# Moving the split of the second attention's query weights on GpSimd behind the first attention's last output product

## The chip, the core and the metric

The kernel runs on one core of a Trainium2 chip. A core has five engines with instruction streams of their own: TensorE (PE, matrix products, with weight loads listed as PEld), VectorE (DVE), ScalarE (ACT), GpSimd (POOL) and SyncE (SP, which issues the DMAs). They meet only in semaphores: an instruction waits until a counter has reached a number. The metric is the device time of one execution in microseconds (us), lower is better; a figure for a kernel is the median of several executions.

## What is computed

Two layers, each a cross attention and a feed-forward block, on 8 sequences of 128 tokens with 128 channels, and a context of the same length with 96 channels. Everything is float32.

```python
def reference(x, ctx_768, ...):
    x = x + _L0_xattn_ref(_layernorm(x), ctx_768, ...)   # 8 heads of 64
    x = x + _L0_ffn_ref(_layernorm(x), Wg, W1, W2, W3)   # 8 experts, top 2, silu(x W1) * (x W2) @ W3
    x = x + _L1_xattn_ref(_layernorm(x), ctx_768, ...)   # 16 heads of 8, with biases
    x = x + _L1_ffn_ref(_layernorm(x), k0, k1, k2, ...)  # three layers of +1/-1 weights
    return x
```

## The kernel before

Every engine has its program written out by hand, in order; there is no scheduler. The tokens lie in `x_sb` as eight blocks of 128 rows, one per sequence, and the blocks make two halves of 512 tokens. A product that needs full precision is made of three passes: weights and activations are each split into a rounded high part and a low rest, and `split3` multiplies high by high, high by low and low by high (lines 478 to 480). Splitting weights is GpSimd's work: a copy that rounds, then a subtraction of the copy from the raw weights.

The first attention (`a_step`) handles the blocks in four pairs, p = 0 to 3. In each step TensorE makes the next pair's queries (lines 478 to 480) and scores (L544), turns the probabilities (L555), multiplies them by the values (L566) and by the output weights (L575, which counts `a_wo` up once per block). VectorE takes the maxima (L1294), divides the probabilities by their sums (L1306) and adds the result to `x_sb` (L1312). ScalarE makes the exponentials (L983). The steps p = 1 and 2 are a hardware loop. `a_q_ps` counts query products, two for each pair, so it reaches 2 * NP = 8 when the last pair's queries are done, early in step p = 2. That is the "third pair" of this document.

Between the first attention and the experts lies the layer norm of both halves. For the first half VectorE seeds the inverse root and GpSimd refines it (`ln_root(1, 0)` on GpSimd, ten operations on 128x4 numbers, L344 to L354). For the second half all of it is on VectorE: moments (L1179), seed (L1186 to L1188), refinement (L1208 to L1215), and the scaling of the four blocks (L1220, `xn`). TensorE then turns them (`ln_transposes(1, 1)`, L485), ScalarE copies the high part (L950), VectorE makes the low part (L1227). On TensorE the order after the last output product is: `b_hidden(0, 0, 0)` (12 products), `gate_logits(0)`, `ln_transposes(1, 1)`, then a wait for `split_w1` at 4, `k1_keys(0)`, six filler products (`keep_clock`, L469), a wait for the second half's low part, `gate_logits(1)`, `k1_keys(1)`, and the experts.

`split_repeated(wq1, wq1_hi, wq1_lo)` is the piece that the change touches. It splits the query weights of the second attention and repeats them in a stacked layout: a rounding copy (L380), a subtraction (L381), and two memsets of 128x128 each (L382, L383). Each waits for the one before through `pool_step`, and the last one raises `split_w1` to 4. The destination is the first attention's own query weights, `wq1_hi, wq1_lo = wq0_hi, wq0_lo`, hence the wait for `a_q_ps` ahead of it. Three places read what it leaves: TensorE's wait before `k1_keys(0)`, VectorE's `stack_bias` (L1285), and the query products of the second attention. In GpSimd's program it stands behind the conversion of the weights `d1_w` and `d2_w` (L424, L425) and ahead of `ln_root(1, 0)`; then comes a wait for `a_wo` at 8, and the split of the third expert's weights (`split_expert`, L415 and L418), which waits for the experts' own progress as well.

Of the kernel before, what the change touches and what calls it, by code (L numbers as in the profile page):

```python
# [27 lines left out]
NP = NB // 2  # L28
# [20 lines left out]
def f32(ap):  # L49

    return ap.bitcast(F32)


def program(nc, a, out):
    with ExitStack() as ctx:
        def sb(name, shape, dt=F32):
            return ctx.enter_context(nc.sbuf_tensor(name, shape, dt))

        def sem(name):
            return ctx.enter_context(nc.semaphore(name))  # L60
# [63 lines left out]
        wq1 = sb("wq1", [C, C])  # L124
        wq1_hi, wq1_lo = wq0_hi, wq0_lo
# [90 lines left out]
        def o_cols(b):  # L216
# [19 lines left out]
        a_q_ps, a_qe, a_qo, a_s, a_max, a_exp, a_pt_ps, a_pt_v, a_pt_a, a_o, a_rs, a_norm, a_oT, a_wo, a_x = (  # L236
            sem("a_" + n) for n in ("q_ps", "qe", "qo", "s", "max", "exp", "pt_ps", "pt_v", "pt_a", "o", "rs", "norm",
                                    "oT", "wo", "x"))
# [14 lines left out]
        def stacked(ap):  # L253

            return ap[:, :].rearrange("c (h d p) -> c h p d", p=NS, d=D1)

        def repeated(ap):

            return ap[:, :].rearrange("c (h d) -> c h d", d=D1).unsqueeze(2).to_broadcast([ap.shape[0], H1, NS, D1])
# [68 lines left out]
        def _(pool):  # L328
            step = [0]

            def chain(ins):

                step[0] += 1
                ins.then_inc(pool_step, 1)
                pool.wait_ge(pool_step, step[0])

            def ln_root(s, t):


                pool.wait_ge(ln_seed, s + 1)  # L340
                bs = slice(4 * t, 4 * t + 4)
                v, y, h, z = ve[:, bs], rs[:, bs], nt[:, bs], nu[:, bs]

                chain(pool.tensor_tensor(h, y, y, ALU.mult))  # L344
                chain(pool.tensor_tensor(h, h, v, ALU.mult))
                chain(pool.tensor_scalar(z, h, -10.0 / 3, None, ALU.add))
                chain(pool.tensor_tensor(z, z, h, ALU.mult))
                chain(pool.tensor_scalar(z, z, 5.0, None, ALU.add))
                chain(pool.tensor_tensor(y, z, y, ALU.mult))

                chain(pool.tensor_tensor(h, y, y, ALU.mult))
                chain(pool.tensor_tensor(h, h, v, ALU.mult))
                chain(pool.tensor_scalar(h, h, -0.5 * 0.375 ** 3, 1.5 * 0.375, ALU.mult, ALU.add))
                pool.tensor_tensor(y, h, y, ALU.mult).then_inc(ln_rs, 1)  # L354
# [24 lines left out]
            def split_repeated(w, hi, lo):  # L379
                chain(pool.tensor_copy(stacked(hi), repeated(w)))  # L380
                chain(pool.tensor_tensor(stacked(lo), repeated(w), stacked(f32(hi)), ALU.subtract))  # L381
                chain(pool.memset(stacked(f32(hi))[:, :, NS - 1, :], 0.0))  # L382
                pool.memset(stacked(f32(lo))[:, :, NS - 1, :], 0.0).then_inc(split_w1, 1)  # L383
# [39 lines left out]
            pool.wait_ge(ld_d, 16 * 6)  # L423
            pool.tensor_scalar(d1_w[:, :, :], k1_u[:, :, :], 2.0, -1.0, ALU.mult, ALU.add).then_inc(d_w, 1)  # L424
            pool.tensor_scalar(d2_w[:, :, :], k2_u[:, :, :], 2.0, -1.0, ALU.mult, ALU.add).then_inc(d_w, 1)  # L425
            pool.wait_ge(a_q_ps, 2 * NP)
            split_repeated(wq1, wq1_hi, wq1_lo)
            ln_root(1, 0)

            pool.wait_ge(a_wo, NB)  # L430

            for buf in range(2):
                split_expert(2 + buf, buf)
# [1176 lines left out]
```

## Time and profile before

| what | value |
|---|---|
| median of 3 runs | 238.93 us |
| lowest and highest | 237.75 and 240.07 us |
| the profiled execution | 237.79 us, of which the span is 235.3 us |
| TensorE busy in the span | 221.6 us (94%) |
| VectorE, ScalarE, GpSimd busy | 165.6, 122.5 and 70.7 us |
| granted TensorE clock, mean | 1.00 |

The span is the time from the first to the last instruction on the chip; the profiled execution took 2.5 us more than its span. Times in the views count from the start of the span. A timeline row gives the start, the length, the engine, the line, the output and its inputs, how many instructions are merged, and in brackets how long the engine had been idle before it and what released it. The chain view follows the work that ended last back through whatever released each piece. "Busy" of an operation runs from when its engine took it up, so time for which it was held while on its engine is inside its length and shows as a longer row, not as idle time.

### The profile page before, as it was taken

To read this page: it belongs to the slowest core of one execution; us is meant where nothing else is said; L and a number is where in the kernel's file an instruction comes from. 1 tells how busy PE (TensorE), PEld (TensorE's weight loads), DVE (VectorE), ACT (ScalarE), POOL (GpSimd) and SP (SyncE) were. 2 spreads that over 40 slices of the span, in tenths; PEclk is the share of its full clock that TensorE was granted. 3 is DMA by queue.
4 is the path that set the end of the run, shared out by engine and by line. 5 is a ranking of instruction groups with operands and counts; after the bars stand their busy time and mean duration, and the time that the engine had idled before them with its cause. 6 is when DMAs were issued, how large, how long until landed. Compare 5 with 4: busy or idle time off the path is not lost.

```text
span 235.3 us, 5028 instructions
## 1 busy us (share of the span) xinstructions
PE 221.6 (94%) x1825; PEld 185.4 (79%) x1825; DVE 165.6 (70%) x429; ACT 122.5 (52%) x292; POOL 70.7 (30%) x105
## 2 busy tenths in 40 slices
PE   8999989798899999999999999999799999989994
PEld 8778879687787888898898889877578887766783
DVE  1688757778767796546555657988878889598763
ACT  2566869688583553323322324164456565757742
POOL 5626599533410215433033900251000000220200
PEclk9999999999999999999999999999999999999999
DMA  6870001000000002202202072000000000000002
GB/s 164 225 197 5 1 3 46 3 0 0 3 0 0 3 1 67 70 0 67 58 9 67 25 198 71 0 4 0 0 3 3 3 0 3 0 3 0 1 0 89
DMA packets 11868, 8.18 MB, mean 35 GB/s; under 512 B 3012, under 2 KB 11144, under 8 KB 11848
## 3 DMA queue, kind: packets, MB, share of 16 engines
q1 hardware_dynamic: 11848, 7.91, 12.6%
q8 instruction: 13, 0.21, 0.4%
q14 instruction: 7, 0.06, 0.1%
HBM read 5.81 MB, written 0.52 MB: 27 GB/s over the span
## 4 chain that ended last, share of the span: by engine, by line
PE 77%; DVE 10%; ACT 8%; issue 2%; POOL 0%; DVEq 0%; ACTq 0%; POOLq 0%
PE ps L676 11%; PE ps L478 9%; PE ps L480 9%; PE ps L850 9%; PE ps L479 9%; ACT probs L983 6%; PE ps L795 3%; PE ps L767 3%; PE ps L754 3%; DVE probs L1306 3%; PE ps L469 3%; PE ps L575 3%; PE ps L474 2%; PE ps L555 2%; PE ps L485 2%
## 5 line engine op out<-in xcount | busy, mean ns | idle before, releaser
L1038 ACT ACTIVATE kT<-ps 128x512 f32<-128x512 f32 x32 | 19.1, 598 | 47.0 <-PE ps L480 47.0
L676 PEld LDWEIGHTS ps<-w,kT 128*128 128x128 f32 x256 | 30.9, 192 | 1.3
L676 PE MATMUL ps<-w,kT 128*128 128x128 f32 x256 | 31.0, 275 | 0.0
L1376 DVE TENSOR_TENSOR kT<-ps,kT 128x512 f32<-128x512 f32 x32 | 21.8, 688 | 11.0 <-PE ps L480 8.7
L1383 DVE SCALAR_TENSOR_TENSOR x_sb<-ps,comb,x_sb 128x128 f32<-128x128 f32 x64 | 18.0, 343 | 13.5 <-PE ps L676 13.5
L478 PE MATMUL ps<-xT_hi,w_hi 128*128 128x512 f32 x64 | 26.5, 414 | 0.8 <-issue 0.6
L480 PE MATMUL ps<-xT_hi,w_lo 128*128 128x512 f32 x64 | 25.2, 394 | 0.0
L479 PE MATMUL ps<-xT_lo,w_hi 128*128 128x512 f32 x64 | 25.0, 391 | 0.0
L983 ACT ACTIVATE probs<-ps,negmax 128x128 f32<-128x128 f32 x64 | 22.6, 410 | 1.8 <-DVE negmax L1294 1.8
L415 POOL TENSOR_TENSOR w_hi<-w_raw,zero 128x512 fp32r<-128x512 f32 x8 | 9.3, 1168 | 46.2 <-DMA w_raw<-in_L_ffn_W 30.9
L1470 DVE TENSOR_REDUCE probs<-ps 128x8 f32<-128x1024 f32 x16 | 19.4, 1222 | 4.8 <-PE ps L754 4.7
L1084 ACT ACTIVATE probsT<-ps 128x1024 f32<-128x1024 f32 x16 | 16.5, 1029 | 9.7 <-PE ps L767 9.7
L460 POOL TENSOR_TENSOR h_a<-kT,h_a 128x512 fp32r<-128x512 f32 x2 | 2.6, 1282 | 46.8 <-ACT kT L1132 46.8
L983 ACT ACTIVATION_READ_ACCUMULATOR probs<-ps,negmax 128x1 f32 x64 | 16.1, 251 | 0.0
L478 PEld LDWEIGHTS ps<-xT_hi,w_hi 128*128 128x128 f32 x64 | 12.1, 188 | 3.2 <-issue 0.7
L480 PEld LDWEIGHTS ps<-xT_hi,w_lo 128*128 128x128 f32 x64 | 12.0, 188 | 2.7
L479 PEld LDWEIGHTS ps<-xT_lo,w_hi 128*128 128x128 f32 x64 | 12.1, 189 | 2.1
L1294 DVE TENSOR_REDUCE negmax<-ps 128x8 f32<-128x1024 f32 x8 | 9.7, 1221 | 5.6 <-PE ps L544 5.6
L1306 DVE TENSOR_TENSOR probs<-probs,rsum 128x1024 f32<-128x1024 f32 x8 | 11.6, 1452 | 0.3
L994 ACT ACTIVATE probsT<-ps 128x512 f32<-128x512 f32 x12 | 6.8, 613 | 9.5 <-PE ps L555 9.5
L754 PE MATMUL ps<-k_st,h_c 32*128 32x128 f32 x128 | 9.8, 276 | 1.4 <-DVE probs L1470 1.3
L555 PE MATMUL ps<-ident,probs 128*128 128x128 f32 x64 | 8.6, 278 | 2.4 <-DVE probs L1306 1.9
(207 smaller groups left out, 511.9 us busy)
## 6 DMA issues: line engine op xcount, KB each, us to landing
w_raw<-in_L_ffn_W SPq DMA_DIRECT2D x16, 128.0 KB, 2.2
k_st<-h_a SPq DMA_DIRECT2D x12, 128.0 KB, 2.7
w<-in_L_ffn_W SPq DMA_DIRECT2D x8, 128.0 KB, 2.2
x_sb<-in_x SPq DMA_DIRECT2D x2, 256.0 KB, 5.1
ctx_sb<-in_ctx SPq DMA_DIRECT2D x2, 192.0 KB, 3.6
w_raw<-in_L_xattn_Wq SPq DMA_DIRECT2D x1, 256.0 KB, 5.1
wo<-in_L_xattn_Wo SPq DMA_DIRECT2D x1, 256.0 KB, 5.0
k_i<-in_L_ffn_k SPq DMA_DIRECT2D x1, 256.0 KB, 3.3
```

The costliest lines, as they stand in the source:

```text
L478: pe.matmul(dst, w_hi, x_hi, start=start, stop=False)
L479: pe.matmul(dst, w_hi, x_lo, start=False, stop=False)
L480: return pe.matmul(dst, w_lo, x_hi, start=False, stop=stop)
L676: ins = pe.matmul(ps[:, 4 + slot, k * C:(k + 1) * C], uT[:, slot, c, k * P:(k + 1) * P], w3[:, buf, c, :], start=(c == 0), stop=(c == NH - 1))
L754: ins = pe.matmul(ps[:, s_bank(b, a) + r % 2, g * P:(g + 1) * P], q_all[rows, g, bs], k_st[rows, g, bs], start=True, stop=True, tile_posit ...
L850: ins = pe.matmul(ps[:, D_BANK[n % ND], :], w_, x_, start=(i == 0), stop=(i == len(terms) - 1))
L983: ins = act.activation(probs[:, j, h, :], ps[:, 2 * j + h % 2, (h // 2) * P:(h // 2 + 1) * P], ACT.Exp, bias=negmax[:, j, h:h + 1], scale= ...
L1038: act.activation(silu[:, c, :], ps[:, c, :], ACT.Silu).then_inc(b_silu, 1)
L1306: dve.tensor_tensor(probs[:, j, :, :], probs[:, j, :, :], rsum[:, j, :].unsqueeze(2).to_broadcast([P, H0, P]), ALU.mult).then_inc(a_norm, 1)
L1376: dve.tensor_tensor(uT[:, slot, c, :], ps[:, 2 + c, :], silu[:, c, :], ALU.mult).then_inc(b_u, 1)
L1383: ins = dve.scalar_tensor_tensor(x_sb[:, b, :], ps[:, 4 + slot, k * C:(k + 1) * C], comb[:, bass.ds(e, 1), b:b + 1].rearrange("p o b -> p ...
L1470: dve.tensor_reduce(top, ps[:, s_bank(b, a):s_bank(b, a) + 2, :].rearrange("p r (g k) -> p r g k", g=NG), X, ALU.max, negate=True).then_in ...
```

## The change

GpSimd's four instructions of `split_repeated` are issued later: `ln_root(1, 0)` comes first, then the wait for `a_wo` at 8 (the last output product of the first attention), then the wait for `a_q_ps`, and then the split, directly ahead of the third expert's split. Nothing is added or removed, and no other engine's program is changed.

```diff
             pool.tensor_scalar(d2_w[:, :, :], k2_u[:, :, :], 2.0, -1.0, ALU.mult, ALU.add).then_inc(d_w, 1)
+            ln_root(1, 0)
+
+            pool.wait_ge(a_wo, NB)
             pool.wait_ge(a_q_ps, 2 * NP)
             split_repeated(wq1, wq1_hi, wq1_lo)
-            ln_root(1, 0)
-
-            pool.wait_ge(a_wo, NB)
 
             for buf in range(2):
                 split_expert(2 + buf, buf)
```

On GpSimd, where the first attention's third pair runs, the difference reads as follows (`wq` are the raw query weights of the second attention, the shapes are those of the output).

```order
 L425 TENSOR_SCALAR d_w<-k_i 128x512
-L380 CAST wq_hi<-wq 128x16x4x8 [waits a_q_ps]
-L381 TENSOR_TENSOR wq_lo<-wq,wq_hi 128x16x4x8 [waits pool_step]
-L382 MEMSET wq_hi 128x128 [waits pool_step]
-L383 MEMSET wq_lo 128x128 [waits pool_step]
 L344 TENSOR_TENSOR nt<-rs 128x4 [waits ln_seed]
 L345 TENSOR_TENSOR nt<-nt,ve 128x4 [waits pool_step]
```

The four are gone from there, so that GpSimd waits for the seed of the first half's layer norm right behind the conversion of the `d` weights. Further down GpSimd's program, behind the last operation of `ln_root(1, 0)`:

```order
 L354 TENSOR_TENSOR rs<-nt,rs 128x4 [waits pool_step]
-L415 TENSOR_TENSOR w_hi<-w_raw,zero 128x512 [waits b_g,ld_up0,a_wo]
+L380 CAST wq_hi<-wq 128x16x4x8 [waits a_q_ps,a_wo]
+L381 TENSOR_TENSOR wq_lo<-wq,wq_hi 128x16x4x8 [waits pool_step]
+L382 MEMSET wq_hi 128x128 [waits pool_step]
+L383 MEMSET wq_lo 128x128 [waits pool_step]
+L415 TENSOR_TENSOR w_hi<-w_raw,zero 128x512 [waits b_g,ld_up0]
 L418 TENSOR_TENSOR w_lo<-w_raw,w_hi 128x512 [waits b_hi]
```

There they now stand behind the wait for `a_wo`, and the third expert's split behind them. VectorE's program at the same point, from its last addition of the first attention on, is the same in both kernels:

```order
L1312 TENSOR_TENSOR x_sb<-ps,x_sb 128x128 [waits a_wo]
L1165 BN_STATS stats<-x_sb 128x6 [waits a_x] x2
L1179 BN_AGGR meanvar<-stats 128x2 [waits ln_st] x4
L1186 TENSOR_SCALAR ve<-meanvar 128x4 [waits ln_mv]
L1187 TENSOR_SCALAR nt<-ve 128x4 [waits ln_nw]
L1188 TENSOR_SCALAR rs<-nt 128x4 [waits ln_nw]
L1208 TENSOR_TENSOR nt<-rs 128x4 [waits ln_nw]
```

What moves is only what GpSimd does beside these rows.

## Rows read from the trace of the kernel before

**Rows 1.** The page (granted clock by slices), and the clock view

```profile
PEclk9999999999999999999999999999999999999999
...
core 0: 235.3 us, clock 1.000
```

**Rows 2.** Chain that ended last, from 45 us (start, length, what)

```profile
50.93 1.94 DVE probs L1306
...
52.92 1.10 PE ps L555 x8
...
54.54 2.70 ACT probs L983 x15
...
74.84 0.70 DVE xT_lo L1227
...
75.59 0.39 PE ps L478
```

**Rows 3.** Timeline of GpSimd, the split in the third pair

```profile
50.85 1.11 POOL L380 CAST wq_hi<-wq 128x512 fp32r<-128x512 f32 x1 [6.31 <-PE ps L480]
52.05 2.20 POOL L381 TENSOR_TENSOR wq_lo<-wq,wq_hi 128x512 fp32r<-128x512 f32 x1
54.30 0.35 POOL L382 MEMSET wq_hi<- 128x128 f32 x1
54.71 0.34 POOL L383 MEMSET wq_lo<- 128x128 f32 x1
```

**Rows 4.** Timeline of VectorE, third pair and the same line undisturbed

```profile
50.93 1.92 DVE L1306 TENSOR_TENSOR probs<-probs,rsum 128x1024 f32<-128x1024 f32 x1
...
57.70 1.23 DVE L1306 TENSOR_TENSOR probs<-probs,rsum 128x1024 f32<-128x1024 f32 x1
```

**Rows 5.** Timeline of TensorE, third pair

```profile
51.58 1.16 PE L544 MATMUL ps<-kT,qo 64*128 64x128 f32 x16
52.92 1.09 PE L555 MATMUL ps<-ident,probs 128*128 128x128 f32 x8 [0.17 <-DVE probs L1306]
```

**Rows 6.** Timeline of TensorE, last output product to second logits

```profile
67.37 1.95 PE L575 MATMUL ps<-wo,qo 128*128 128x128 f32 x16
...
73.41 0.76 PE L485 MATMUL ps<-ident,xn 128*128 128x128 f32 x4
73.93 0.47 PE L478 MATMUL ps<-ctxT_hi,h_c 97*128 97x512 f32 x1
...
74.71 0.78 PE L469 MATMUL ps<-ones 128*128 128x128 f32 x6
```

**Rows 7.** Timeline of VectorE, second half's normalisation

```profile
70.68 0.17 DVE L1186 TENSOR_SCALAR ve<-meanvar 128x4 f32<-128x4 f32 x1
...
72.67 1.12 DVE L1220 TENSOR_SCALAR xn<-x_sb,meanvar,rs 128x128 f32<-128x128 f32 x4
```

**Rows 8.** Timeline of GpSimd, a split at the start

```profile
8.71 0.60 POOL L376 CAST wq_hi<-w_raw 128x512 fp32r<-128x512 f32 x1
9.39 1.28 POOL L377 TENSOR_TENSOR wq_lo<-w_raw,wq_hi 128x512 fp32r<-128x512 f32 x1
```

**Rows 9.** Timeline of VectorE beside it

```profile
9.98 0.72 DVE L1186 TENSOR_SCALAR ve<-meanvar 128x4 f32<-128x4 f32 x1
```

**Rows 10.** Timeline of GpSimd, an expert's split amid the second pair

```profile
39.82 1.28 POOL L418 TENSOR_TENSOR w_lo<-w_raw,w_hi 128x512 fp32r<-128x512 f32 x1
```

**Rows 11.** Timeline of VectorE beside it

```profile
39.87 2.32 DVE L1306 TENSOR_TENSOR probs<-probs,rsum 128x1024 f32<-128x1024 f32 x1
```

**Rows 12.** Timeline of GpSimd, a memset beside VectorE's small operation

```profile
34.27 0.95 POOL L407 MEMSET ctxT_lo<- 1x1024 f32 x1
```

**Rows 13.** Timeline of VectorE beside it

```profile
35.01 0.20 DVE L1304 RECIPROCAL rsum<-sums 128x8 f32<-128x8 f32 x1
```

**Rows 14.** Busy time in stretches (length, PE, PEld, DVE, ACT, POOL, clock, DMA)

```profile
40.00:44.00 4.00, 3.12 (x41) 2.60 (x41) 3.95 (x4) 1.80 (x5) 3.91 (x3) 1.00 0.20 62
```

**Rows 15.** Timeline of TensorE, its first matmuls

```profile
0.98 3.67 PE L469 MATMUL ps<-ones 128*128 128x128 f32 x16 [0.98 <-POOL ones L362]
```

## The prediction

> **What bounds the kernel now.** I began with the page and the clock view: TensorE is granted its full clock (1.00, which is 2.4 GHz) in the whole span [rows 1], so a time that TensorE loses is a wait and not a slower clock. Next I read the chain that ended last around the two places where GpSimd's split stands before and after the change. In the third pair it goes through VectorE's division of the probabilities (L1306, 1.94 us), TensorE's turning of them and ScalarE's exponentials [rows 2]. Behind the first attention's last output product it ends in the low part of the second half's layer norm (L1227 at 74.84), which releases TensorE at 75.59 [rows 2]. So at both places VectorE stands on the path, and TensorE, which is the busy engine between them, waits for it. GpSimd is on neither path. What counts is what its work does to VectorE's.
>
> That it does something is plain in the timelines. GpSimd's split begins at 50.85, VectorE's division 0.08 later. The division takes 1.92 us where the same instruction beside an idle GpSimd takes 1.23 [rows 3, 4]. The effect goes the other way as well: GpSimd's subtraction (L381) is taken up at 52.05, while VectorE divides until 52.85, and takes 2.20 us in all [rows 3, 4]. Whoever comes first keeps the other out, apparently for the whole instruction. A subtraction of GpSimd that began at 39.82 and ended at 41.10 stretched a division begun at 39.87 to 2.32 us [rows 10, 11]. Most important here, the same happens to a tiny VectorE instruction: L1186, 128x4 numbers, elsewhere 0.17 us, took 0.72 at the start of the program, from 9.98 to 10.70, and GpSimd's subtraction beside it ended at 10.67 [rows 7 to 9].
>
> **What the change takes away.** The hold of the division in the third pair: 1.92 - 1.23 = 0.69 us on VectorE. On TensorE it is worth far less. TensorE had the next pair's scores to do until 51.58 + 1.16 = 52.74, and it sat idle only 0.17 us before it turned the probabilities at 52.92 [rows 5]. So the gain is 0.17 us. Bounds: nothing, if ScalarE's exponentials at 54.54 [rows 2] are held by something else, and 0.69 if TensorE's modelled ends hide more. I take 0.2, the idle time that the trace names. GpSimd's own wait for the seed of `ln_root(1, 0)` gains nothing: it had finished the split at 54.71 + 0.34 = 55.05 [rows 3], before the third pair itself was through.
>
> **What it brings in.** The last output product ends at 67.37 + 1.95 = 69.32 [rows 6]. With 0.08 us for the signal, GpSimd's copy starts at 69.40. It lasts 1.11, the subtraction follows 0.09 later, at 70.60, and needs 1.40 by itself (from the end of the division at 52.85 to its own end at 54.25 [rows 3, 4]), so it runs to 72.00. The memsets, 0.35 and 0.34 with gaps of 0.05, run from 72.05 to 72.80. VectorE in the meantime does its last addition and the statistics and comes to L1186 at 70.68 [rows 7], which is 0.08 us behind the start of the subtraction. As in [rows 8, 9] it then ends some 0.03 us behind the subtraction, at 72.03 in place of 70.85: a delay of 1.18 us.
>
> Does TensorE feel it? Everything VectorE does from there to L1227 is one chain of small steps. The last `xn` is ready at 72.67 + 1.12 = 73.79, and TensorE's four turnings [rows 6, 7] end at 73.41 + 0.76 = 74.17, so the last of them followed its operand at once. Then come ScalarE's copy, L1227 and TensorE at 75.59. The only work that TensorE has for the gap is `k1_keys(0)` at 73.93 and the filler to 74.71 + 0.78 = 75.49 [rows 6], and both stand behind the turning in its program, so they are late as well. The experts behind them are a nearly unbroken stream of products, so no later wait gives the time back. I let all 1.18 through; at most 0.1 of it could vanish in TensorE's lead.
>
> Bounds for this hold: at the short end the copy takes only the 0.60 of the plain copy at 8.71 [rows 8], so that the subtraction ends at 71.49 and the delay is 0.67; below that nothing at all, if VectorE slips in between. At the long end VectorE's next two steps, L1187 and L1188, are held by the two memsets too, 0.35 and 0.34 more, which makes 1.87.
>
> What lies beside other work: the wait for `split_w1` ahead of `k1_keys(0)` is met at 72.80, and TensorE was there at 73.93 [rows 6]. That leaves 1.1 us of margin, and more once TensorE is late; `stack_bias` on VectorE comes later still. On GpSimd nothing is queued behind the split but the third expert's split, which also waits for the second group of the experts' products, that is for work behind the gap. SP's queue is untouched.
>
> **The sum.** -0.2 + 1.2 = +1.0 us. The profiled execution took 237.79 (span 235.3 and 2.5 around it), so its own successor would take 238.8. That execution lies at the low end of the three runs and 1.1 us below their median. Against the median of 238.93 I forecast 239.9 us.
>
> **A rule against the row.** The memsets are where I choose. A reciprocal of VectorE (L1304) at 35.01 was not lengthened (0.20 us) though a memset of GpSimd ran from 34.27 to 35.22 [rows 12, 13]; I therefore leave the memsets out. The Trainium skill, "SBUF — State Buffer", section "SBUF: two separate sides", says that GpSimd and VectorE share one pair of ports as an exclusive lock that the first comer holds for its whole instruction, and that a VectorE operation in a two-port mode is shut out by any GpSimd operation. [...] The trace agrees on the first part [rows 4, 9, 11]. By the second part a reciprocal proves nothing for L1187 and L1188, which are scalar operations like L1186, and the sum would be +1.7.
>
> **The rivals.**
>
> *The memsets hold too.* VectorE's next step starts 0.03 us behind L1186, at 72.06, and the first memset at 72.05, so it is a matter of who comes first. Price 1.87 - 0.2 = +1.7, giving 240.6. For it speaks L1186 itself [rows 9], against it the reciprocal [rows 13].
>
> *VectorE is not held.* If the copy starts or ends so that L1186 to L1215 fall into a gap, or if the small operations finish first and GpSimd does the waiting, then only the removed hold counts: -0.2, giving 238.7. Against it: GpSimd's work is nearly solid from 69.40 to 72.80, VectorE's small steps lie in the middle of it, and the trace has one of them caught [rows 9].
>
> *The hole cools TensorE: slower.* TensorE's wait between the first logits and the turning grows by 1.2 us, in a stretch that holds six filler products already [rows 6]. If its clock fell to the lower level of 1.2 GHz there, the experts' first products would run at half pace. At the very start, from 0.98, sixteen filler products of 128 columns took 3.67 us, 0.23 each, where six at 74.71 took 0.78, 0.13 each [rows 6, 15]. If such a slow stretch lasted as long as the filler did, 3.7 us, it would cost about half of that, and twice as long a stretch all of it: 1.0 + 1.8 to 3.7, so 241.7 to 243.6. It decides from the point at which the granted clock drops in that slice. Against it: between 40 and 44 us TensorE was busy for only 3.12 of 4 us and was still granted 1.00 [rows 14], and here the new idle time is of that size.
>
> **How the numbers follow.** Forecast (one hold, +0.5 to +1.2): 0.6. Memsets as well: 0.18. No hold: 0.14. Slower clock: 0.05. Something unnamed: 0.03. The cases that hold most of the chance reach from 238.7 to 240.6. The three runs of the kernel before lie within 1.2 us to either side of their median, and a median of the changed kernel can move by some part of that, so I take 238.3 to 241.2. About 1%, 2.4 us here, is what a measurement of this kernel can tell from no change. No case but the clock's reaches that by itself; the scatter of the runs can lift the memset case over it now and then. That makes slower by over 1% 0.12, within 1% 0.84, and faster by over 1% 0.04.
>
> **What the changed profile would show.** L1306 of the third pair at 1.23 us and TensorE's idle time of 0.17 before L555 gone. L380 starting 0.1 us behind the end of the eighth L575 group and L381 around 1.4 us long. L1186 of the second half at about 1.3 us in place of 0.17; a longer L1187 or L1188 would speak for the memsets. TensorE idle some 1 us around L485, and the distance from the end of L575 to `gate_logits(1)` grown from 75.59 - 69.32 = 6.3 to about 7.4 us, with the granted clock still 1.00. I am wrong if L1186 stays at 0.17, if that distance stays while L1186 grows (then TensorE had work to put into the gap), or if the difference lies in another stage altogether.

## The result and the profile after

| | median | executions | lowest to highest |
|---|---|---|---|
| before | 238.95 us | 20 | 237.24 to 250.72 us |
| changed | 239.98 us | 20 | 239.01 to 242.85 us |

The ratio is 1.0072, 95% interval 1.0044 to 1.0099: slower by 0.4 to 1.0%, or 1.7 us on 238.9. The forecast was 239.9 us (range 238.3 to 241.2) with slower by 1.0. Time and direction hold; measured by the ratio, the sum of the terms was 0.7 us short.

Half or more of the executions of either kernel run at a mean granted clock of about 0.993 and take some 1.6 to 2 us longer than those at 1.000, so beside each ratio, which leaves out executions more than 1.5% above the fastest of their kernel, I give the median of those at 1.000. It is 237.56 us for the kernel before (13 executions, run beside the first four experiments) and 239.39 for the changed one (10): +1.8. The plain medians of the table differ by only 1.0, since they mix the two clocks. That the forecast of 239.9 lies 0.1 from 239.98 is therefore partly luck.

The changed kernel was profiled in an execution of 239.39 us (span 237.4), at full clock, as the one before was (237.79).

VectorE's timeline has both places. Columns as in [rows 4, 7].

```profile
51.32 1.23 DVE L1306 TENSOR_TENSOR probs<-probs,rsum 128x1024 f32<-128x1024 f32 x1
...
70.28 0.48 DVE L1165 BATCH_NORM_STATS2 stats<-x_sb 128x6 f32<-128x128 f32 x2
70.67 0.36 DVE L1179 BATCH_NORM_AGGREGATE meanvar<-stats 128x2 f32<-128x6 f32 x4
71.07 1.47 DVE L1186 TENSOR_SCALAR ve<-meanvar 128x4 f32<-128x4 f32 x1
72.57 0.35 DVE L1187 TENSOR_SCALAR nt<-ve 128x4 int32<-128x4 int32 x1
72.96 0.35 DVE L1188 TENSOR_SCALAR rs<-nt 128x4 int32<-128x4 int32 x1
73.34 0.16 DVE L1208 TENSOR_TENSOR nt<-rs 128x4 f32<-128x4 f32 x1
```

GpSimd beside it:

```profile
69.77 1.11 POOL L380 CAST wq_hi<-wq 128x512 fp32r<-128x512 f32 x1 [3.71 <-PE ps L575]
70.96 1.55 POOL L381 TENSOR_TENSOR wq_lo<-wq,wq_hi 128x512 fp32r<-128x512 f32 x1
72.57 0.33 POOL L382 MEMSET wq_hi<- 128x128 f32 x1
72.96 0.33 POOL L383 MEMSET wq_lo<- 128x128 f32 x1
```

TensorE, in the third pair and behind the last output product:

```profile
53.31 1.06 PE L555 MATMUL ps<-ident,probs 128*128 128x128 f32 x8 [0.17 <-ACT probsT L994]
...
67.75 1.95 PE L575 MATMUL ps<-wo,qo 128*128 128x128 f32 x16
...
75.12 1.10 PE L485 MATMUL ps<-ident,xn 128*128 128x128 f32 x4 [1.17 <-DVE xn L1220]
...
77.64 0.40 PE L478 MATMUL ps<-xT_hi,wg_hi 128*8 128x512 f32 x1
```

What to see. In the third pair L1306 takes 1.23 us instead of 1.92 [rows 4], as it should, but TensorE starts to turn the probabilities after the same 0.17 us of idle time as before [rows 5]; only the name of the releaser has changed, from VectorE to ScalarE's L994. At the second place L1186 starts 0.11 us behind GpSimd's subtraction and ends at 72.54, 0.03 behind the subtraction's end at 72.51, as at the start of the program [rows 8, 9]. L1187 and L1188 end 0.02 behind the end of a memset each. Not every small step is held: the statistics and moments (L1165, L1179), which read SBUF too, lie beside GpSimd's copy (69.77 to 70.88) and take 0.48 and 0.36 us, as in the kernel before. From the start of L1186 to the start of L1208 it is 2.27 us. The three steps at 0.17 with gaps of 0.03 to 0.04 take 0.62 (as in the kernel before and in e1 below), so the delay is 1.65. TensorE now waits 1.17 us for the first `xn`, with gaps inside the four turnings besides (1.10 us against 0.76 [rows 6]). From the end of the last output product, 67.75 + 1.95 = 69.70, to the second gate logits at 77.64 it is 7.94 us, against 75.59 - 69.32 = 6.27 before [rows 2, 6]. I call this **the distance** from here on. It grew by 1.67 us. The spans differ by 2.1; the remaining 0.4 lies ahead of both places: TensorE turns the third pair's probabilities at 53.31 against 52.92 already [rows 5]. It is scatter and not the change: the first turning of the first pair is late by 0.3 as well (25.84 against 25.52), before GpSimd comes to anything that was moved, and in e10 below, which has the changed order of GpSimd, the third pair's turning stands at 53.01.

### The profile page after: what moved, and what is told of

Same layout as the page of the kernel before. It is cut to its first block, busy times and chain, and to the rows that moved or that the text cites. A ratio compares the mean times of both kernels' runs of the same rounds, so it can differ in the third digit from the quotient of the medians.

```text
span 237.4 us, 5029 instructions
## 1 busy us (share of the span) xinstructions
PE 223.0 (94%) x1825; PEld 186.3 (78%) x1825; DVE 166.9 (70%) x429; ACT 122.7 (52%) x292; POOL 70.2 (30%) x105
## 4 chain that ended last, share of the span: by engine, by line
PE 75%; DVE 12%; ACT 10%; issue 2%; POOL 0%; DVEq 0%; ACTq 0%; POOLq 0%
PE ps L676 11%; PE ps L478 9%; PE ps L850 9%; PE ps L480 8%; PE ps L479 8%; ACT probs L983 7%; PE ps L795 3%; PE ps L767 3%; PE ps L754 3%; PE ps L474 2%; PE ps L555 2%; PE ps L469 2%; DVE probs L1306 2%; PE ps L485 2%; PE ps L780 2%
## 5 line engine op out<-in xcount | busy, mean ns | idle before, releaser
L994 ACT ACTIVATE probsT<-ps 128x512 f32<-128x512 f32 x12 | 6.8, 614 | 9.4 <-PE ps L555 9.4
L1306 DVE TENSOR_TENSOR probs<-probs,rsum 128x1024 f32<-128x1024 f32 x8 | 10.9, 1361 | 0.3
```

## The experiments

The theory: GpSimd and VectorE shut each other out, one whole instruction at a time. The changed kernel puts GpSimd's split beside the small steps of the second half's layer norm, all of them on TensorE's path, and takes it from a place where the hold cost nothing. Rivals: a cost of GpSimd's work in that stage that is not this exclusion; the memsets holding nothing; a loss in another stage; the clock. All distances, with the ratio to the kernel before, which ran on the same chip beside each:

| kernel | distance | ratio, 95% interval | median at full clock (before, beside it) |
|---|---|---|---|
| before | 6.27 us | | |
| changed | 7.94 | 1.0072, 1.0044 to 1.0099 | 239.39 us (237.56) |
| e1 split among the experts | 6.27 | 1.0016, 0.9979 to 1.0053 | 237.38 (237.56) |
| e2 memsets away | 7.55 | 1.0054, 1.0018 to 1.0091 | 238.88 (237.56) |
| e3 memsets alone | 6.54 | 1.0025, 0.9991 to 1.0058 | 237.95 (237.56) |
| e4 second pair freed too | 6.27 | 0.9988, 0.9954 to 1.0022 | 236.89 (237.56) |
| e5 subtraction in four | 7.17 | 1.0025, 0.9988 to 1.0063 | 238.25 (237.77) |
| e6 subtraction twice | 8.78 | 1.0236, 1.0172 to 1.0300 | none (237.77) |
| e7 queries in the hole | 6.27 | 0.9932, 0.9897 to 0.9966 | 237.07 (237.77) |
| e8 e4 and e7 together | 6.28 | 0.9874, 0.9812 to 0.9937 | 236.03 (237.77) |
| e9 behind the chain | 6.28 | 1.0027, 0.9987 to 1.0068 | 237.50 (237.26) |
| e10 lowered waits only | 7.94 | 1.0064, 1.0025 to 1.0103 | 239.48 (237.26) |
| e11 e6 with filler | 8.79 | 1.0109, 1.0038 to 1.0180 | 239.65 (237.38) |

The full-clock medians of e1, e3, e5, e8, e9 and e11 stand on one to three executions each, and so does the 237.38 beside e11; where they and the ratio disagree in size, the distances in the traces decide.

**e1, the split where VectorE only works on PSUM.**

```diff
 # from the kernel before
-            pool.wait_ge(a_q_ps, 2 * NP)
-            split_repeated(wq1, wq1_hi, wq1_lo)      # amid the third pair
...
+            split_repeated(wq1, wq1_hi, wq1_lo)      # behind the experts' splits
             pool.memset(top_w, 0.0).then_inc(zeros_ok, 1)
 # and the lowered waits: k1_keys(0) and stack_bias wait for split_w1 at 3,
 # c_queries(0) for split_w1 at 4
```

> The split is issued behind the experts' weight splits, where VectorE's operations all have one operand in PSUM, and the three waits that need less than the whole split are lowered to what they read. It collides with VectorE at neither of its two earlier places. Theory (the whole loss is VectorE held by GpSimd at the second half's layer norm, and the hold in the third pair cost nothing): the distance from the end of the last output product to the second gate logits is 6.3 us again, L1186 0.17 us, and the time equals the kernel before within 0.1 us (ratio 1.000), with TensorE's 0.17 us idle before L555 of the third pair still there, though L1306 takes 1.23. Rival, the term of the forecast (the hold in the third pair cost 0.2 us): 0.2 us faster than the kernel before. Rival, the loss comes from somewhere else than from the split beside that layer norm (a later stage that GpSimd's order disturbs): still slower than the kernel before by some 1 us or more.

Of the three waits, only the query products read the split weights; `k1_keys(0)` and `stack_bias` need what the first three counts of `split_w1` stand for, so that they can be released earlier. e10 below tests that lowering by itself.

The timelines of VectorE and TensorE in e1:

```profile
50.95 1.22 DVE L1306 TENSOR_TENSOR probs<-probs,rsum 128x1024 f32<-128x1024 f32 x1
...
70.68 0.17 DVE L1186 TENSOR_SCALAR ve<-meanvar 128x4 f32<-128x4 f32 x1
70.89 0.17 DVE L1187 TENSOR_SCALAR nt<-ve 128x4 int32<-128x4 int32 x1
```

```profile
52.94 1.06 PE L554 MATMUL ps<-ident,probs 128*128 128x128 f32 x8 [0.17 <-ACT probsT L994]
```

Distance 6.27, all small steps at 0.17, and full-clock executions of 237.38 us against 237.56, the lowest 237.26 against 237.24. The loss is gone with the split, and the third pair's idle time of 0.17 us stays although its hold is gone. The 0.2 us that the forecast credited there do not exist: behind VectorE's division stood ScalarE's second copy (L994), which frees the bank that the turning writes. In the kernel before it ended at 51.69 + 1.08 = 52.77, the division at 52.85, and TensorE started at 52.92:

```profile
51.69 1.08 ACT L994 ACTIVATE probsT<-ps 128x512 f32<-128x512 f32 x2 [0.28 <-PE ps L555]
```

**e2, copy and subtraction there, memsets away, and e3, the reverse.**

```diff
 # both with the lowered waits; e2, from the changed kernel: split_repeated without its memsets, and
+            clear_last(wq1_hi, wq1_lo)               # the two memsets, behind the experts' splits
 # e3, from the kernel before: the same cut, the memsets at the layer norm
             pool.wait_ge(a_wo, NB)
+            pool.wait_ge(ln_mv, 2 * NB)
+            clear_last(wq1_hi, wq1_lo)
```

> As the changed kernel, but its two memsets go behind the experts' splits; the copy and the subtraction stay behind the last output product. Theory (each memset holds one more VectorE step): L1186 stays at 1.47 us, L1187 and L1188 fall from 0.35 to 0.17 us, the distance from the last output product to the second logits falls from 7.9 to 7.6 us: 1.3 us slower than the kernel before, 0.35 faster than the changed one. Rival (L1187 and L1188 are late for another reason, for instance the semaphore traffic of two engines): they stay at 0.35, and the distance at 7.9.

> Copy and subtraction stay in the third pair as in the kernel before; only the two memsets stand at the second half's layer norm, released by the end of its moments (L1179). Theory (a memset alone shuts out VectorE's small scalar operations for as long as it runs): one or two of L1186 to L1188 take about 0.35 in place of 0.17 us, together 0.2 to 0.5 us more, and the time is that much above the kernel before. Rival (a memset reads nothing and so holds nothing, as beside the reciprocal at 35.01): all three stay at 0.17 and the time is the kernel before's.

VectorE in e2, where lines have moved by four (L1190 to L1192 are L1186 to L1188 here):

```profile
70.89 1.45 DVE L1190 TENSOR_SCALAR ve<-meanvar 128x4 f32<-128x4 f32 x1
72.38 0.17 DVE L1191 TENSOR_SCALAR nt<-ve 128x4 int32<-128x4 int32 x1
72.58 0.17 DVE L1192 TENSOR_SCALAR rs<-nt 128x4 int32<-128x4 int32 x1
```

VectorE and GpSimd in e3 (L1191 to L1193):

```profile
70.74 0.17 DVE L1191 TENSOR_SCALAR ve<-meanvar 128x4 f32<-128x4 f32 x1
70.94 0.26 DVE L1192 TENSOR_SCALAR nt<-ve 128x4 int32<-128x4 int32 x1
71.23 0.35 DVE L1193 TENSOR_SCALAR rs<-nt 128x4 int32<-128x4 int32 x1
```

```profile
70.83 0.35 POOL L384 MEMSET wq_hi<- 128x128 f32 x1 [5.09 <-DVE meanvar L1184]
71.23 0.33 POOL L385 MEMSET wq_lo<- 128x128 f32 x1
```

Both as the theory has it. In e2 the memsets' share is gone, 7.94 - 7.55 = 0.39 us. In e3 L1191, which started before the first memset, is not held; the other two end 0.02 us behind a memset. So a memset, which reads nothing, does shut out these scalar operations, and 0.27 us of it arrive at TensorE. It costs less than its length: a step that would take 0.17 anyway and ends with the memset at 0.35 loses 0.18.

**e9, the same stage but behind the chain, and e10, a control.**

```diff
 # e9, from the changed kernel, with the lowered waits; e10 has the lowered waits alone
             pool.wait_ge(a_q_ps, 2 * NP)
+            pool.wait_ge(ln_xn, 2 * NB)
             split_repeated(wq1, wq1_hi, wq1_lo)
```

> The changed kernel, with GpSimd's split released by the last scaled block of the second half (L1220) in place of the last output product, and the three waits for it lowered as in e1. The split thus runs some 4 us later, still in the same stage, beside VectorE's operations on PSUM (L1227, L1376). Theory (only the collision with VectorE's small steps costs): L1186 to L1188 at 0.17, the distance from the last output product to the second logits 6.3 us, TensorE's idle time before L485 gone, and in executions at full clock the time of the kernel before, 237.6 us. Held without harm, at most: L1280, which is off the path. Rival (any work of GpSimd in this stage costs, by semaphores or otherwise): the distance stays above 7 us and the time above 239.

> The changed kernel with nothing but the three lowered waits that e1, e2 and e9 also have. A control. Theory: they cost and bring nothing, since TensorE reaches k1_keys(0) after the split is done in any case: distance 7.9 us, the changed kernel's time, 239.4 us in executions at full clock. Rival (the lowered waits are what made e1 and e2 faster than the changed kernel): below 239.

The trace of e9 is 1.3 us late from the first pair on (26.80 against 25.52), ahead of the edit, so its rows compare by their distance. In it GpSimd starts here, and of VectorE's operations only L1282 (L1280 before, 0.27 us there) is held:

```profile
75.22 1.10 POOL L380 CAST wq_hi<-wq 128x512 fp32r<-128x512 f32 x1 [8.29 <-DVE xn L1222]
76.39 1.55 POOL L381 TENSOR_TENSOR wq_lo<-wq,wq_hi 128x512 fp32r<-128x512 f32 x1
```

```profile
71.94 0.17 DVE L1188 TENSOR_SCALAR ve<-meanvar 128x4 f32<-128x4 f32 x1
...
76.72 1.28 DVE L1378 TENSOR_TENSOR kT<-ps,kT 128x512 f32<-128x512 f32 x2
77.91 0.50 DVE L1282 TENSOR_SCALAR bq_r<-bq,sign 2x128 fp32r<-2x128 f32 x1
```

Distance 6.28. The whole split, some 4 us of GpSimd's time in the same stage, costs nothing if it misses the chain; two VectorE operations with one operand in PSUM (L1378, 128x512) run beside it at their usual length. The ratio of e9, 1.0027, includes no difference. e10 repeats the changed kernel: 7.94 and 1.0064. The lowered waits are not the cause.

**e5 and e6, the size of the instruction.**

```diff
 # e5: four subtractions of four heads each      # e6: the whole one, twice
+                for q in range(4):
+                    hs = slice(4 * q, 4 * q + 4)
+                    chain(pool.tensor_tensor(stacked(lo)[:, hs], repeated(w)[:, hs], ...
```

> The changed kernel with its subtraction cut into four instructions of four heads each; GpSimd's work there becomes some 0.2 us longer. Theory (each GpSimd instruction shuts out one VectorE step for its own length, and VectorE takes one step between two of them): no step is held for 1.3 us any more. L1186, L1187, L1188 and L1208 take about 0.4 to 0.5 us each, the last ones of the chain 0.16 again. VectorE gets six steps through in GpSimd's stream instead of three, so the distance from the last output product to the second logits falls from 7.94 to some 7.6 to 7.8 us. Rival (a pool of bandwidth shared in proportion to what is read): VectorE's steps read 4 numbers a row, so that cutting the subtraction changes nothing: L1186 about 1.4 as before, or all of them 0.17.

> The changed kernel with the subtraction issued twice in a row. Theory (whole instructions, first comer): L1186 is held by the first, L1187 by the second subtraction, 1.4 to 1.5 us each, L1188 by the first memset (0.35). The distance from the last output product to the second logits grows from 7.94 to about 9.1 us, and the time by the same 1.2. L1208, which has two operands in SBUF, meets the second memset, which reads nothing: by the rule of the Trainium skill, SBUF - State Buffer, section on the two sides, it is not held and takes 0.16; by a lock without exemption it takes 0.35. Rival (TensorE's late arrival is set by something other than VectorE's chain): the time does not follow.

VectorE in e5 (L1188 to L1213 are L1186 to L1211), with GpSimd's four pieces in one row:

```profile
71.08 0.45 DVE L1188 TENSOR_SCALAR ve<-meanvar 128x4 f32<-128x4 f32 x1
71.56 0.17 DVE L1189 TENSOR_SCALAR nt<-ve 128x4 int32<-128x4 int32 x1
71.77 0.38 DVE L1190 TENSOR_SCALAR rs<-nt 128x4 int32<-128x4 int32 x1
72.18 0.16 DVE L1210 TENSOR_TENSOR nt<-rs 128x4 f32<-128x4 f32 x1
72.38 0.37 DVE L1211 TENSOR_TENSOR nu<-nt,ve 128x4 f32<-128x4 f32 x1
```

```profile
70.98 2.36 POOL L383 TENSOR_TENSOR wq_lo<-wq,wq_hi 128x128 fp32r<-128x128 f32 x4
```

VectorE, GpSimd and TensorE in e6 (L1187 to L1210 are L1186 to L1209):

```profile
70.90 1.47 DVE L1187 TENSOR_SCALAR ve<-meanvar 128x4 f32<-128x4 f32 x1
72.40 0.17 DVE L1188 TENSOR_SCALAR nt<-ve 128x4 int32<-128x4 int32 x1
72.60 1.38 DVE L1189 TENSOR_SCALAR rs<-nt 128x4 int32<-128x4 int32 x1
74.02 0.16 DVE L1209 TENSOR_TENSOR nt<-rs 128x4 f32<-128x4 f32 x1
74.22 0.16 DVE L1210 TENSOR_TENSOR nu<-nt,ve 128x4 f32<-128x4 f32 x1
```

```profile
70.79 3.17 POOL L382 TENSOR_TENSOR wq_lo<-wq,wq_hi 128x512 fp32r<-128x512 f32 x2
74.02 0.33 POOL L383 MEMSET wq_hi<- 128x128 f32 x1
```

```profile
75.80 1.10 PE L486 MATMUL ps<-ident,xn 128*128 128x128 f32 x4 [2.02 <-DVE xn L1221]
...
78.31 0.60 PE L479 MATMUL ps<-xT_hi,wg_hi 128*8 128x512 f32 x1
```

That the first comer shuts the other out is confirmed, and that the hold lasts as long as its instruction, by holds of 0.2 to 0.3 us when the pieces are small and 1.3 and 1.2 when there are two large ones. Two expectations missed. Between two subtractions the order was not one VectorE step for each GpSimd instruction but two, one held and one free. A held step ends 0.02 to 0.03 us behind GpSimd's instruction and the next one starts 0.03 later; GpSimd, which waits for its own completion, starts again 0.05 to 0.1 us behind its own end. So both come back at nearly the same moment, and here VectorE got in first. This is no rule: in the changed kernel both started at 72.57, and at 72.96, as printed, and there the memset won each time. The lead of VectorE is why e5 gained more than expected: four holds, 0.28 and three times 0.21 (the fourth on L1213), make 0.9, and the distance is 6.27 + 0.90 = 7.17. The memsets of e5 come at 73.40 and 73.78, beside steps with two operands in SBUF, and hold none of them. In e6 the second hold falls on the third step instead of the second, and the memset then meets L1209 and L1210. These have two operands in SBUF, and stay at 0.16 us through a memset that runs from 74.02 on. In e5 the same L1210, there L1211, was held (0.37) by a piece that reads. So the exemption in the Trainium skill, "SBUF — State Buffer", section "SBUF: two separate sides", holds here: two operands in SBUF are shut out by GpSimd work that reads SBUF, not by a memset, while scalar operations like L1186 to L1188 are shut out by both. The forecast had set that section against its own choice to leave the memsets out, and the section was right.

e6 was slower than the lengthened distance says: 244.57 us, where 2.5 us more than 237.8 would be 240.3. The windows view shows why (columns: window, length, busy times of TensorE, its loads, VectorE, ScalarE and GpSimd, granted clock, DMA):

```profile
74.00:78.00 4.00, 2.20 (x13) 1.72 (x13) 2.68 (x12) 1.06 (x2) 0.65 (x2) 1.00 0.00 0
78.00:82.00 4.00, 3.90 (x12) 2.58 (x12) 2.48 (x6) 0.59 (x1) 0.00 (x0) 0.57 0.02 4
82.00:86.00 4.00, 4.00 (x29) 3.31 (x28) 2.52 (x26) 2.24 (x5) 0.86 (x1) 1.00 0.00 0
```

Behind 2.02 us of idle TensorE the mean clock from 78 to 82 us was 0.57, which is the lower level of 1.2 GHz most of the time, and the second gate logits and the first products behind them took 0.43 us apiece, from start to start, instead of 0.23. This is the slower rival of the forecast, at a hole of 2.0 us and not at that of 1.17. It is not the whole of the 4.3 us between 240.3 and 244.57: the same profile shows 0.61 between 173 and 177 us, a later loss that is told under e4, e7 and e8.

**e11, filler in that hole.**

```diff
             gate_logits(0)
+            keep_clock(9, 4)                         # 18 filler products
             ln_transposes(1, 1)
```

> The kernel of e6 (subtraction twice), with 18 filler products of 128 columns on TensorE between the first gate logits and the second half's turning, where e6 left it idle for 2.0 us. In e6 all four executions ran at a mean granted clock of 0.979 to 0.986, and its profile shows 0.57 between 78 and 82 us. Theory (that idle stretch is what the clock fell for): with the filler the clock is 1.00 there, the distance from the last output product to the second logits stays 8.8 us, since VectorE's chain sets it, and executions at full clock take 237.4 + 2.5 = 239.9 us, some 4 us less than e6. Rival (the clock in e6 fell for another reason, such as what came before the stretch): still about 0.57 in that stretch, and 244 us.

```profile
78.00:82.00 4.00, 3.90 (x22) 2.86 (x23) 2.58 (x9) 1.18 (x2) 0.00 (x0) 1.00 0.00 0
```

The clock stays, with VectorE's chain as late as in e6: the last output product starts at 67.35 and the second gate logits at 78.09, which is a distance of 8.79. The median falls from 244.57 to 241.28, and the one execution at full clock took 239.65, close to what the distance says (8.79 - 6.27 = 2.5 above 237.38). The idle stretch was the cause. The later loss is in the profile of e11 as well (mean clock 0.993), so the 3.3 us between the medians are the price of the one at 78 us; the two profiled executions differ by 1.9 us (spans 241.3 and 239.4).

**e4, e7 and e8, a version that beats both.** Two things found on the way: the second pair's hold [rows 10, 11] is one that TensorE does feel (0.88 us idle), and the executions at 0.993 that were profiled (e1, e4, e5, e11) lose their clock right behind a hole of TensorE at about 168 us. e1 is shown here, and is back at 1.00 from 173 us on; L753 is the second attention's score product:

```profile
169.28 0.85 PE L753 MATMUL ps<-k_st,h_c 32*128 32x128 f32 x8 [1.30 <-DVE probs L1470]
```

```profile
165.00:169.00 4.00, 2.98 (x45) 2.11 (x44) 3.08 (x4) 2.14 (x3) 0.00 (x0) 1.00 0.00 0
169.00:173.00 4.00, 3.72 (x15) 3.02 (x16) 2.11 (x3) 0.80 (x2) 0.00 (x0) 0.58 0.01 4
```

```diff
 # e4, on top of e1
+            pool.wait_ge(a_norm, 4)
             split_expert(1, 1)
...
-            pool.tensor_scalar(d1_w[:, :, :], ...
             pool.tensor_scalar(d2_w[:, :, :], ...
+            pool.wait_ge(a_norm, 6)
+            pool.tensor_scalar(d1_w[:, :, :], ...
 # e7, from the kernel before; e8 is e4 with it
+                if s == 1:
+                    c_queries(NG + 2)
                 if s + 2 < NB:
                     c_scores(s + 2, 0)
                 if s == 1:
-                    c_queries(NG + 2)
                     c_queries(NG + 3)
```

> The split among the experts as in e1, and besides the second expert's weight split waits for the second pair's last division, the conversion of the d1 weights for the third pair's, so that none of them meets a division of VectorE. Theory: L1306 of the second pair falls from 2.32 to 1.23 us, TensorE's idle time ahead of L555 there from 0.88 to the 0.17 us that ScalarE's copy of the turned probabilities sets, so 0.7 us faster than the kernel before (ratio 0.997). Rival (behind every hold stands another wait of the same length, as in the third pair): the idle time does not fall, and the time equals the kernel before's.

> The kernel before, with one group of the second attention's query products (c_queries(6)) moved ahead of c_scores(3, 0) on TensorE, into the 1.3 us that TensorE is idle at 168 us. It has to do with the scatter of the runs: executions with a mean granted clock of 1.000 take 237.6 us in the median, those with about 0.993 take 239.2, and in a profile of such a one the clock is lower from about 169.5 to 172.8 us, right behind this hole. Theory (that hole is what lets the clock fall in part of the executions): the granted clock is 1.000 in nearly all executions, their median falls by 1.6 us, and the products that fill the hole give another 0.9 us: 236.7 in full-clock executions, ratio of all about 0.991. Rival (the clock falls on account of TensorE's load before, not of the hole): the share of executions at the lower clock stays near 60%, and only the 0.9 us is gained.

> e4 and e7 together: the split among the experts, nothing of GpSimd's beside the second pair's division, and the query products in the hole at 168 us. Theory: the terms add up, 0.7 + 0.9 us in full-clock executions and the lower clock gone besides, 236.0 us against 237.6, ratio of all about 0.988. Rival (the shift by 0.7 us changes where the hole falls, and the clock falls somewhere else): the time is that of e7 or above it.

The second pair in e4 (L1308 is the division, L556 the turning):

```profile
40.34 1.22 DVE L1308 TENSOR_TENSOR probs<-probs,rsum 128x1024 f32<-128x1024 f32 x1
```

```profile
42.00 1.06 PE L556 MATMUL ps<-ident,probs 128*128 128x128 f32 x8 [0.17 <-ACT probsT L996]
```

The division is at 1.22 us and the idle time at 0.17, the same floor of ScalarE's copy. Full-clock executions take 236.89 us, 0.7 less than before, as expected (four of them, spans 234.7 to 234.9 against 235.4 to 235.6 in most of the kernel before); the ratio, 0.9988, does not tell it from no change. In e7 the score product waits this long:

```profile
169.44 0.66 PE L754 MATMUL ps<-k_st,h_c 32*128 32x128 f32 x8 [0.16 <-DVE probs L1471]
```

e7 behaves as expected in 10 of its 12 executions: the hole is down from 1.3 to 0.16 us, 9 of the 10 are at a full clock of 1.000 and the tenth at 0.998, the gain at full clock is 0.7 us (0.9 was expected), and the ratio over these ten is 0.9932. But the other two took 257 and 258 us at a mean clock of 0.905, and with them the mean of all twelve is 240.6 us, against 238.7 for the kernel before. Three of the seven of e8 did the same, and there the granted clock of the profiled one, by fortieths of the span, reads

```profile
PEclk9999999999999999999999999997555555599999
```

which is half speed (0.5 is 1.2 GHz) in seven of 40 slices and a lowered clock in the one ahead of them, from about 175 to 223 us. Of the kernel before, one execution of 104 was anything like it (250.72, its clock is not on record), and none of the changed kernel and the other experiments. e8 is 1.3% faster than the kernel before in the remaining four, and I would not put it in its place: whether filling the hole brings the long loss of clock about was not settled, and why it would is open; five of 19 against one of 104 is a strong hint that it does. e4 is what I would keep.

## Why the prediction was right, and where it was off

- **What bounds the stage, and who waits for whom: right.** The chain goes through VectorE at both places, and TensorE passed the whole delay on: 1.65 us on VectorE, 1.67 on TensorE. "I let all 1.18 through" was the right step at the wrong size.
- **The hold by the subtraction, 1.18 us: measured 1.30** (1.47 - 0.17). The subtraction lasts 1.55 us with nothing in its way (e2, e9 and e10 show the same), not the 1.40 that I had counted from the end of a division in the third pair. "Apparently for the whole instruction" was a little too strong: 54.25 - 1.55 = 52.70, so that subtraction had begun 0.15 us before the division ended. The divisions show it too. That of [rows 11] ends 1.09 us later than its own 1.23 would have it, where the subtraction beside it still had 1.23 to run, and that of the third pair was held for 0.69 us, where the copy still had 1.03.
- **The memsets, left out: they hold**, 0.35 us of the 1.65. Here a sentence on the reciprocal [rows 12, 13] outvoted L1186 itself. That row could hardly have shown a hold: the memset had 0.21 us left when the reciprocal began, so a held reciprocal would have ended at 35.24 instead of 35.21. It was of another kind of operation besides, and the kind matters, as L1165 and L1179 beside the copy show; whether a longer memset holds a reciprocal, no run shows. The rival priced the hold at 0.35 and 0.34; it is 0.18 each, since a step of 0.17 is contained in the memset's length. This rival's mechanism is what happened. That its total of +1.7 came out to the tenth is luck: the memsets were 0.34 too dear, the subtraction 0.12 too cheap, and a gain of 0.2 was taken off that does not exist.
- **The gain in the third pair, 0.2 us: nothing** (e1). The 0.17 us of idle time had two enders, and the view names only the last. This is the lower bound that I had given.
- **The rival that VectorE is not held: wrong**, in every run of the split at that place (changed, e2, e5, e6, e10, e11).
- **The clock: right that it stays** in the changed kernel (1.00 in its profile in that stage), and right in kind that a larger hole costs it (e6, e11). Its price there, e6 against e11, is 3.3 us between the medians and 1.9 between the profiled executions, inside the 1.8 to 3.7 that I had put on it.
- **The range** held, because its ends were taken from the memset case and the runs' scatter. The point within it, 239.9, met the plain median by a sum that was 0.7 us short and a median that mixes two clocks.

## What to carry to other kernels

A work package moved to an idle stretch of GpSimd is not hidden there if VectorE has a chain of small scalar or two-operand SBUF operations beside it: each may wait out the rest of a GpSimd instruction, whatever its own size. Compare the lengths of the same line at several places; one that is longer by the rest of a neighbour's instruction is a hold, and it is worth removing only where TensorE's idle time behind it has no second ender. Put such packages beside VectorE work on PSUM (e1, e9), or cut them into short instructions (e5), and before rejecting a second, smaller hold check that the row against it is of the same kind of operation and long enough to have shown the hold.

## What the runs showed of the hardware that I had not expected

- Even an integer shift on 128x4 numbers (L1187) is shut out by a memset: 0.35 us instead of 0.17.
- The statistics and moments of the layer norm (L1165, L1179) were not held by a GpSimd copy, though they read SBUF; the scalar steps right behind them were.
- Between chained GpSimd subtractions two VectorE steps go through each time, one held and one free (e5, e6, e11). Beside the memsets of the changed kernel and of e3 it was one, and held: both engines are back at nearly the same moment, and a few hundredths of a us decide.
- In the profiles of e1, e4, e5, e6 and e11, an idle time of TensorE of 1.3 us in a loosely filled stretch is followed by a few us at a lower clock; in those of the kernel before, the changed one, e2, e3, e9 and e10 the same idle time is not. By the mean clock some such loss happens in about six of ten executions of the kernel before (52 of the 84 for which the clock is listed are below 1.000), at a cost of about 1.7 us. Filled (e7), nine of ten were at 1.000. With an idle time of 2.0 us ahead of it (e6), the mean clock was 0.979 to 0.986 in four of four.
